# Turning 13 normalised tiles as squares on VectorE, with a trip through DRAM, instead of on TensorE

## The reference, cut to what matters

```python
# x (2048, 512) float32, adj (2048, 2048)
n = layernorm(x)
q, k, v = n @ W_q.T + b_q, n @ W_k.T + b_k, n @ W_v.T + b_v
z = (q @ k.T) / sqrt(512) * adj
attn = softmax(where(z == 0, -10000, z), axis=1)
x = x + relu(attn @ v)
m = layernorm(x)                       # the rows that the change is about
r = softmax(m @ Wr)                    # router, 8 experts; the two best are kept
w = softmax(top_2(r))
shared = (silu(m @ Wg_s) * (m @ Wu_s)) @ Wd_s
special = sum over the 2 picked experts e of w_e * (silu(m @ Wg[e]) * (m @ Wu[e])) @ Wd[e]
out = x + shared + special
```

## Time and profile before

| what | us |
|---|---|
| median of 3 runs | 1375.9 |
| the profiled execution's own time | 1377.3 |
| its span, first to last instruction | 1375.6 |
| TensorE busy | 1365.6 |
| TensorE weight loads | 1177.3 |
| VectorE busy | 909.2 |
| ScalarE busy | 453.6 |
| GpSimd busy | 196.9 |

### The profile page before, as it was taken

How to read it: one execution, slowest core, us unless ns; L and a number is a source line. 1 busy time by engine, 2 the same in 40 slices (tenths; PEclk the granted TensorE clock), 3 DMA queues, 4 the chain that set the end, 5 groups by cost and what they waited for, 6 DMA issues and landing times.

```text
span 1375.6 us, 19783 instructions
## 1 busy us (share of the span) xinstructions
PE 1365.6 (99%) x6720; PEld 1177.3 (86%) x6720; DVE 909.2 (66%) x1957; ACT 453.6 (33%) x702; POOL 196.9 (14%) x234
## 2 busy tenths in 40 slices
PE   9999999999999999999999999999999999999998
PEld 7888888888888878898989889898898989888887
DVE  7957767767777767465576747566475736367874
ACT  4522212212212245342343424234242525243331
POOL 3500112212211321011011110201102020100000
PEclk9999999999999999999999999999999999999999
DMA  5916565466466564462616133361435252553101
GB/s 183 259 46 169 163 185 165 148 187 168 153 175 191 175 237 147 154 175 55 206 31 215 31 106 124 54 207 34 124 107 152 83 155 98 148 151 107 47 16 61
DMA packets 114420, 185.47 MB, mean 135 GB/s; under 512 B 13776, under 2 KB 47568, under 8 KB 114336
## 3 DMA queue, kind: packets, MB, share of 16 engines
q1 hardware_dynamic: 98064, 153.43, 35.5%
q0 software_dynamic: 9760, 18.93, 7.0%
q10 hardware_dynamic: 6528, 12.22, 3.1%
HBM read 129.82 MB, written 55.77 MB: 135 GB/s over the span
## 4 chain that ended last, share of the span: by engine, by line
PE 91%; DVE 3%; DMA 3%; issue 2%; ACT 1%; SPq 0%; POOL 0%; DVEq 0%; ACTq 0%; POOLq 0%
PE bank L307 83%; PE bank L1042 5%; DMA turned<-p_moved 1%; DMA p_moved<-turned 1%; PE bank L874 1%; PE bank L1033 1%; DMA early_x<-x2t 0%; ACT sc L1210 0%; PE bank L798 0%; PE bank L752 0%; DVE fill L1602 0%; DVE pT_l L1457 0%; PE bank L868 0%; DVE turned L1620 0%; SPq L459 0%
## 5 line engine op out<-in xcount | busy, mean ns | idle before, releaser
L1846 DVE TENSOR_TENSOR hid<-bank,hid 128x384 f32<-128x384 f32 (+1 forms) x80 | 46.8, 584 | 176.6 <-PE bank L307 176.4
L307 PE MATMUL bank<-dn_h,hT_h 128*128 128x512 f32 x320 | 125.7, 393 | 0.2 <-DVE hT_l L1457 0.2
L307 PE MATMUL bank<-dn_h,hT_l 128*128 128x512 f32 x320 | 125.7, 393 | 0.0
L307 PE MATMUL bank<-dn_l,hT_h 128*128 128x512 f32 x320 | 125.6, 392 | 0.0
L307 PE MATMUL bank<-xq_h,gate_h 128*128 128x384 f32 (+1 forms) x320 | 111.3, 348 | 0.1
L307 PE MATMUL bank<-xq_h,gate_l 128*128 128x384 f32 (+1 forms) x320 | 111.2, 348 | 0.0
L307 PE MATMUL bank<-xq_l,gate_h 128*128 128x384 f32 (+1 forms) x320 | 110.8, 346 | 0.0
L307 PE MATMUL bank<-xq_h,up_h 128*128 128x384 f32 (+1 forms) x320 | 110.7, 346 | 0.0
L307 PE MATMUL bank<-xq_h,up_l 128*128 128x384 f32 (+1 forms) x320 | 110.4, 345 | 0.0
L307 PE MATMUL bank<-xq_l,up_h 128*128 128x384 f32 (+1 forms) x320 | 110.4, 345 | 0.0
L1128 ACT ACTIVATE hT_h<-hid 128x384 fp32r<-128x384 f32 (+1 forms) x96 | 53.8, 561 | 164.2 <-DVE hid L1846 124.7
(11 more groups left out here) (278 smaller groups left out, 3294.8 us busy)
## 6 DMA issues: line engine op xcount, KB each, us to landing
gate_raw<-in_L_ffn_Wg_dram SPq DMA_DIRECT2D x16, 1024.0 KB, 5.5
up_raw<-in_L_ffn_Wu_dram SPq DMA_DIRECT2D x16, 1024.0 KB, 10.2
dn_raw<-in_L_ffn_Wd_dram SPq DMA_DIRECT2D x16, 1024.0 KB, 12.5
sc<-in_adj_dram SPq DMA_DIRECT2D x30, 512.0 KB, 6.1
p_moved<-turned SPq DMA_DIRECT2D x30, 512.0 KB, 3.0
turned<-p_moved SPq DMA_DIRECT2D x120, 128.0 KB, 5.4
x_t<-in_x_dram SPq DMA_DIRECT2D x24, 256.0 KB, 4.8
slots<-x2row ACTq DMA_DIRECT2D x12, 512.0 KB, 4.4
```

Of the source, the lines that this page charges most:

```text
L307: mm = pe.matmul(o, lhs(a, c), rhs(b, c), start=first and n == 1, stop=last and n == 3 * len(chunks))
L1846: dve.tensor_tensor(hid[:, c % 2, 0:w], bank[2 + c % 2][:, 0:w], hid[:, c % 2, 0:w], ALU.mult).then_inc(sem("hid"), 1)
```

## The change

For the 13 tiles that steps 1 to 13 finish, TensorE's four transposes and the copy out of bank 7 go. In their place:

- VectorE turns each 32x32 square of `x2row` in place of its own (`turn_row`, one 128x512 transpose instruction), behind `row_normalised`, into `x2_squares`;
- SP stores `x2_squares` to DRAM (`x2_moved`), waits until it has landed and until x1 is stored, and reads it back in four DMAs with the squares in transposed order into `x2_banks` (`move_rows`);
- ScalarE copies `x2_banks` into `x2T` (`join_turned`): before the exponential in odd steps, behind it in even ones.

The logits on TensorE go behind the first `attend` group in odd steps and behind the second in even ones. On VectorE, `logits` in even steps goes behind the second `scaled_queries`, and `picks` behind the last `queries_low`; in odd steps the first `low` goes ahead of `ranks` and the first `fill_zeros`. The store of `x2T` goes from `store` into `move`, between the stores and the reads of the probabilities. In step 14 `picks` goes ahead of `first_pieces` on VectorE. In step 15 `count_picks` goes behind the first `attend` and `turn`, and VectorE's `residual` and `row_normalised` go ahead of `take_counts` and `ranks`. The last outputs share one semaphore.

```diff
 SP
-            def move(i):
+            def move(i, stored=False):
...
+                if stored:
+                    store_turned(i - 2)
                 for h in range(2):
                     sp.wait_ge(sem(f"p_half{h}"), MOVED * i + 16)
...
+            def move_rows(i):
+                sp.wait_ge(sem("row_turned"), i + 1)
+                sp.dma_start(x2_moved, x2_squares[:].rearrange("p a c q -> p (a c q)")).then_inc(sem("row_moved"), 16)
+                sp.wait_ge(sem("x1_out"), 16 * (i + 1))
+                sp.wait_ge(sem("row_moved"), MOVED * i + 16)
+                by_bank = x2_moved.rearrange("(i r) (a f) -> a r i f", i=BANKS, a=BANKS)
+                for a in range(BANKS):
+                    sp.dma_start(x2_banks[Q * a:Q * a + Q, :, :, :].rearrange("p i c q -> p i (c q)"), by_bank[a]
+                                 ).then_inc(sem("row_moved"), 16)
...
             def attention_step(i, b):
                 fetch(i, b)
+                stored = not isinstance(i, int) or i > 0
+                if stored:
                     store(i - 1)
-                move(i + 1)
+                    move_rows(i - 1)
+                move(i + 1, stored)
 TensorE
             def route_logits(i):
                 wait(pe, "x2T_done", i)
+                wait(pe, "counts_read", i - 1)
...
                 if last:
-                    count_picks(i - 1)
                     attend(i, 0, last)
                     turn(2)
+                    count_picks(i - 1)
...
-                if prev:
+                if split:
                     turn_normalised(i, b)
                 scores(i + 1, 1 - b, 3)
-                if prev:
+                if split:
                     route_logits(i)
...
                 attend(i, 0)
+                if prev and b == 1:
+                    route_logits(i)
                 attend(i, 1)
+                if prev and b == 0 and not split:
+                    route_logits(i)
 ScalarE
+            def join_turned(i):
+                wait(act, "row_moved", MOVED * i)
+                copy(x2T[:].rearrange("p c (i q) -> p i c q", q=Q), x2_banks[:]).then_inc(sem("x2T_done"), 1)
...
+                short = b == 1 or split
+                if split:
                     keep_turned(i)
+                elif prev and short:
+                    join_turned(i)
                 probabilities(i + 1, 1 - b)
-                if prev:
+                if prev and short:
                     router_exp(i)
+                if prev and not short:
+                    join_turned(i)
...
                 if prev:
+                    if not short:
+                        router_exp(i)
                     pick_exp(i)
 VectorE
+                wait(dve, "x2T_done", min(i - 1, ROWS) if isinstance(i, int) else i - 1)   # in output
...
+            def turn_row(i, b):
+                wait(dve, "x2_done", i)
+                wait(dve, "logits", i - 1)
+                wait(dve, "x2t_out", 16 * (i - 1))
+                dve.transpose(x2_squares[:], x2row[1 - b][:].rearrange("p (c a q) -> p a c q", a=BANKS, q=Q)
+                              ).then_inc(sem("row_turned"), 1)
...
                     row_normalised(i, b)
+                    if not split:
+                        turn_row(i, b)
...
+                if b == 1:
+                    low(i, 0)
                 if counted:
                     ranks(i - 1)
                 fill_zeros(i + 1, 1 - b, 0)
-                low(i, 0)
+                if b == 0:
+                    low(i, 0)
...
-                if prev:
+                short = b == 1 or split
+                if prev and short:
                     logits(i)
                 if ahead:
                     scaled_queries(2 * j + 2, 0)
                 if split:
+                    picks(i)
                     first_pieces(0, 2)
                 else:
                     turn_squares(i + 1)
                 if ahead:
                     queries_low(2 * j + 2, 0)
                     scaled_queries(2 * j + 3, 1)
-                if prev:
-                    picks(i)
+                if prev and not short:
+                    logits(i)
                 if ahead:
                     queries_low(2 * j + 3, 1)
+                if prev and not split:
+                    picks(i)
```

More of the change, by code:

```diff
@@ L61, in gnn_moe @@
     p_moved = nc.dram_tensor("p_moved", [2, P, BANKS * HALF * Q], F32, kind="Internal").ap()
+    x2_moved = nc.dram_tensor("x2_moved", [P, BANKS * D // BANKS], F32, kind="Internal").ap()
     x2t = nc.dram_tensor("x2t", [T, DC * P], F32, kind="Internal").ap()
@@ L93, in gnn_moe @@
         x2T = at("x2T", 194 * K, [P, DC, P])
+        x2_squares = at("x2_squares", 194 * K, [P, BANKS, DC, Q])
+        x2_banks = at("x2_banks", 192 * K, [P, BANKS, DC, Q])
         x2row = [at("x2row0", 196 * K, [P, D]), at("x2row1", 200 * K, [P, D])]
@@ L262, in gnn_moe @@
         LAST_O = bank[3]
+        ROWS = NT - 3
         TURNED = 2 * (NT - 1)
@@ L464, in store, with store_turned @@
                 sp.dma_start(rows(acc, i), x1[:]).then_inc(sem("x1_out"), 16)
+            def store_turned(i):
                 sp.wait_ge(sem("x2T_done"), i + 1)
@@ L469, in attention_step @@
                 fetch(i, b)
-                if not isinstance(i, int) or i > 0:
+                stored = not isinstance(i, int) or i > 0
+                if stored:
                     store(i - 1)
-                move(i + 1)
+                    move_rows(i - 1)
+                move(i + 1, stored)
             move(0)
@@ L481, in _ @@
             store(NT - 3)
+            store_turned(NT - 3)
             def load_turned(o, b, name):
@@ L520, in _ @@
             store(NT - 2)
+            store_turned(NT - 2)
             sp.wait_ge(sem("attended"), 4 * NT)
@@ L526, in _ @@
             store(NT - 1)
+            store_turned(NT - 1)
             sp.wait_ge(sem("sent"), 64 * NT)
@@ L618, in _ @@
                     sp.wait_ge(sem("z_done"), 4 + 4 * n + k + 1)
-                    sp.dma_start(rows(out, 8 + 4 * n + k), z[:, n, k, :]).then_inc(sem(f"out{n + 1}"), 16)
-            sp.wait_ge(sem("out"), 16)
+                    sp.dma_start(rows(out, 8 + 4 * n + k), z[:, n, k, :]).then_inc(sem("out"), 16)
+            sp.wait_ge(sem("out"), 16 + 2 * 64)
             sp.wait_ge(sem("out0"), 64)
-            sp.wait_ge(sem("out1"), 64)
-            sp.wait_ge(sem("out2"), 64)
         @block.gpsimd
@@ L1222, in last_group @@
                 copy(pT["h"][:, 4 * g:4 * g + 4, :].rearrange("p k q -> p (k q)"), bank[4 + g % 2][:]).then_inc(sem("pT_h"), 1)
+            def join_turned(i):
+                wait(act, "row_moved", MOVED * i)
+                copy(x2T[:].rearrange("p c (i q) -> p i c q", q=Q), x2_banks[:]).then_inc(sem("x2T_done"), 1)
             def keep_turned(i):
-                wait(act, "x2_turned", i)
+                wait(act, "x2_turned", i - ROWS)
                 wait(act, "logits", i - 1)
@@ L1322, in next_tokens @@
                     if b < 2:
-                        act.wait_ge(sem("x2_turned"), NT + q + 1)
+                        act.wait_ge(sem("x2_turned"), NT - ROWS + q + 1)
                         copy(o[:, :, part], bank[(c + 1) % 2 if b == 0 else 7][:].rearrange("p (c q) -> p c q", c=DC)).then_inc(sem("xq_h"), 1)
@@ L1656, in row_normalised @@
             def row_normalised(i, b):
-                wait(dve, "x2_turned", i - 2)
+                if isinstance(i, int) and i - 2 > ROWS:
+                    dve.wait_ge(sem("x2_turned"), i - 2 - ROWS)
+                else:
+                    wait(dve, "row_turned", i - 2)
                 normalise(x2row[1 - b][:], x1[:], NT + i, 1 - b).then_inc(sem("x2_done"), 1)
+            def turn_row(i, b):
[4 more added lines that the diff above has]
+                              ).then_inc(sem("row_turned"), 1)
             def logits(i):
@@ L1717, in attention_step @@
                     output(i, b)
+                    residual(i, b, j + b)
                     take_counts(i - 1)
+                    row_normalised(i, b)
                     ranks(i - 1)
-                    residual(i, b, j + b)
                     last_group(2)
-                    row_normalised(i, b)
                     last_group(3)
```

1 line of the change is left out of this document (removed).

## The result

The changed kernel takes 1379.2 us in the median (16 runs, 1378.3 to 1382.2), beside 1376.55 for the kernel before in 16 runs (1374.7 to 1377.9). The ratio is 1.0021, with an interval of 1.0014 to 1.0028. It is 2.65 us slower where 0.6 faster was forecast, so 3.25 us of the forecast have to be explained. The forecast was 1375.3, with a range of 1372.5 to 1378.5, and was set against the 1375.9 that three runs of the kernel before had given; its median of 16 is 0.65 higher. The profiled execution took 1378.7 with a span of 1377.0, that is 1.4 more than before in both.

What follows compares the result with a forecast made beforehand. TensorE was taken to bound the kernel, with VectorE at 97% of the bound and taking over after the change. +1.7 + 0.9 - 1.9 - 1.3 = -0.6 us gave 1376.7 profiled, 1375.3 in the runs' measure, range 1372.5 to 1378.5.

Steps and rivals of the forecast that it cites:

- who becomes the bound: Attention loop: VectorE becomes the bound, its pair of steps 53.37 us against 52.87 before, TensorE's 51.75.
- The turn: VectorE in each loop step: the added transpose costs 0.75 us, bounds 0.55 and 0.9; two make 1.5 a pair.
- The late logits of even steps: VectorE in even steps: small reads and picks no longer fill waits, costing 0.80 us, bounds 0.35 and 1.1.
- the number 51.07 for VectorE alone: Attention loop before the change: VectorE's pair without its waits for TensorE, 52.87 - 1.8 = 51.07 us.
- in odd steps the first `low` only changes places: 0 on VectorE: VectorE in odd steps: moving the first low part of the probabilities costs 0 us, lower bound -0.2.
- until the output at 175.66 its slack covers the additions, and TensorE's saving of about 0.9 shows: First loop steps: VectorE's slack of 1.66 us covers additions of 1.55, so TensorE's saving of about 0.9 shows.
- the end: Step 14 to the experts: picks save 1.9 us, the x2T store adds 0.9, no half clock saves 1.3.
- I take no fall: TensorE near 490: standing about 1.4 us does not lower its clock, so the half-clock stretch goes.
- The second, probabilities too late in odd steps: Rival, 18%: odd steps' `low` waits for late probabilities, some 5 us on top of the forecast, 1380.3 us.
- The third: Rival, 5%: x2T in odd steps later than 16 us after the output makes TensorE the bound again; 1382.3 us.
- The first, that VectorE doesn't take over: Rival, 25%: most of TensorE's 7.6 us saving comes through; 1365.1 us, or about 1370.5 with a 52.3 us pair.
- TensorE's idle of some 8 us: Sign in the attention: TensorE's idle rises to some 8 us, at odd steps' logits or at the outputs' release.

Runs made afterwards that it cites:

- double_turn: The changed kernel, with VectorE making each of the 13 transposes twice; 1389.0 us, 1.0094 of the kernel before.
- more_tensor: The changed kernel, with four unread TensorE transposes of a constant added in each of steps 1 to 13; 1379.8 us, 1.0024 of the kernel before.
- picks_first: low_back, with even steps' logits ahead of the first `queries_low`, `picks` ahead of the second, `router_exp` between ScalarE's two `queries`; 1375.1 us, 0.9982 of the kernel before.
- low_back: The changed kernel, with the odd step's first `low` back behind `ranks` and the first `fill_zeros`; 1377.0 us, 1.0002 of the kernel before.
- end_alone: The kernel before, with only the change's edits to steps 14 and 15; 1373.8 us, 0.9973 of the kernel before.
- after: The changed kernel as first profiled, against the kernel before; profiled execution 1378.7 us, median 1379.2, ratio 1.0021.
- odd_alone: The changed kernel with only odd steps' seven tiles turned the new way, even steps' the old, `low` at its old place; 1378.3 us, 1.0006 of the kernel before.
- odd_keep: odd_alone, with ScalarE's copy into x2T between the two high parts of the probabilities in even steps; 1370.8 us, 0.9954 of the kernel before.

## Why the prediction was wrong

**Right: who becomes the bound.** The mechanism of the forecast came true, and double_turn and more_tensor show it from both sides. The turn costs VectorE 0.76 us: before, the mask started 0.09 ahead of the end of x2row, now it starts 341.32 - 340.65 = 0.67 behind it; 0.75 was forecast. The late logits of even steps cost 0.79: from the queries (384.04) to the picks (386.22) it is 2.18, less 0.60 for the low part that now stands there, less the 0.79 from 328.19 to 328.98; 0.80 was forecast. Behind this stood the number 51.07 for VectorE alone. It closes: 53.60 less 1.42 for two turns (double_turn), less 0.52 (picks_first), less 0.25 (low_back) is 51.41, and the two reads of the logits and the new wait (0.35 + 0.06, from the rows) bring it to 51.0; with the first turns at their 0.76 it is 50.9.

**Wrong, the first failed step: "in odd steps the first `low` only changes places: 0 on VectorE".** It cost 0.23 us in each odd step; I had 0 and a bound on the side of a gain only. I had priced the instruction and not its neighbours. Whether an operation overlaps the one in front depends on what that is: the same `fill` starts 0.08 before the end of a low part and 0.12 after the end of an accumulator's reading. With the 0.06 of the new wait, and the even step 0.05 shorter, this is the pair's 53.60 instead of 53.37.

**Wrong, the second: "until the output at 175.66 its slack covers the additions, and TensorE's saving of about 0.9 shows".** It implies an output at 174.8. It came at 175.34, without a wait for TensorE in front of it. TensorE's saving did not show in step 1 either: its next output came at 146.59, against 146.50 before. In step 2 the transpose itself waited 0.52 us (151.19) for the store of x2T to have left the SBUF; I had listed that wait in the diff and given it no price, though I had moved the store behind the reads of the rows. This closes step 2. Before, it took 29.16 us, with 1.66 of slack at the output and 0.85 at the second mask, which waited 0.76 there (I had counted only the first). That leaves 26.65; with 1.55 added and the wait of 0.52 it is 28.72, and it took 28.75. The first of the five pairs took 54.00, 0.4 more than the others, and the last odd step grew by 0.18 where I had nothing.

The sum for step 14's head is 0.6 + (268.41 - 5 x 53.37 = 1.6) + 0.2 = 2.3 above the forecast's 1.6 (1.7 with the added wait), and it came at +3.9. That lies inside the bounds that I had written down (-2.7 to +4.6); the terms that I had put at nothing all came out on the slow side.

**Right in size, wrong in its terms: the end.** From step 14's output to the experts I had 40.11 - 1.9 + 0.9 - 1.3 = 37.8, and it is 37.56. The runs take it apart. With the end's edits alone it is 36.19 (end_alone): 3.9 less, where I had 1.9 + 1.3 = 3.2. With the loop's edits on top and no slow stretch it is 36.44 (low_back): 0.25 more, where I had 0.9 for the store of x2T. The 0.9 had too little behind it: step 14's second high part came 0.5 later than before, but no less late in end_alone, where the store stood at its old place. The last 1.1 is between low_back and after, and here "I take no fall" of the clock failed: TensorE waited 1.70 us for x2T at 478.64, and the 3.4 us behind it ran at 0.50, which costs 1.6 at the rate of the matmuls there (0.43 apart instead of 0.23). That the total came near is luck: a saving too small, a cost too large and a fall left out.

I had only asked whether the old wait of TensorE at 490 would shrink. I had not asked what TensorE does in step 14 once VectorE is late. It goes ahead, and its copy stays where ScalarE's queue has it. The wait for x2T there follows this lead from run to run. With the turn 6.38 us after the output (end_alone) there is none; with 5.79 (odd_alone) it is 0.71, with 5.49 (picks_first) 1.09, with 5.40 (low_back) 1.14, with 4.57 (after) 1.70, with 4.56 (more_tensor) 2.13. The second high part starts at 8.05 to 8.46 in all of them. That the lead makes the wait is read from these six profiles; no run changes the lead alone. The Trainium skill's rule in "DMA: Bandwidth & Descriptors", section "Queues, rings and completion order", that each DMA engine takes descriptors in ring order, fits the store's landing, which went from 2.1 to 6.8 us; I had applied the rule to the rows alone. The late landing is what step 2's transpose waited for.

**The median.** 1.25 us of the miss is not in the two profiles. 0.75 of it is that the profiled execution of before lay above its median. The rest is scatter of the changed kernel, whose executions differ in how long they stay at the lower clock behind the waits for x2T (3.41 us in one profile at 480, 6.83 in the other, and the profile beside the forecast is the one with the shorter). low_back, picks_first and odd_keep have no such stretch in their profiles, and all their executions have a mean granted clock of 0.999 or more; double_turn, with waits for x2T of 1.5 to 1.9 us, has them in five steps and a mean of 0.99 to 0.997. That shorter waits are the reason is an argument from these profiles and not shown; low_back still waits 1.14 at that place.

**The rivals.** The second, probabilities too late in odd steps, did not occur. ScalarE had the first high part at 340.20, 3.66 us after the output, against 3.46 before, and `low` ran at 342.61 without a wait. The third didn't either: x2T was there at 348.26, 11.7 us after the output, where I had 13.9. The first, that VectorE doesn't take over, is excluded by more_tensor. Of the signs, TensorE's idle of some 8 us came (9.9 us of its weight loads' waits for x2T), but the long ones, 1.35 us and more, stand in even steps and in step 14, where I had looked for them in odd ones.

## What to carry to other kernels

When an engine stands at 97% of the bound, take its whole dependent chain over one period, subtract only its waits on others, and price each edit by the gap it makes or closes to both neighbours; an instruction moved without a change costs something if it leaves an overlap. Compare what is moved with the slack that is there: here half of the tiles fitted into it and all of them did not. On the engine that copies for the bound, put the copy ahead of whatever waits for a DMA. Where an edit makes one engine late, the other comes early: ask what that one will wait for at the next place where it leads. And time an edit's neighbours without it, since here 3.4 of the 6.4 us came from the end's edits alone.

## What the runs showed of the hardware

- A 128x512 fp32 transpose in 32x32 squares takes VectorE 0.71 us, and two in a row, with a wait of the second for the first, 1.46 (double_turn).
- Not every wait brings TensorE's clock down. After waits of 0.97 (327.81) and 1.70 us (478.64) about 3.4 us ran at 1.2 GHz; after 1.14 us in low_back, 1.11 in odd_alone's even step, and 1.64 in the setup of before, it stayed at 2.4. The same code can do both: in odd_alone it fell after 1.13 (137.74), in after it stayed behind a wait of 0.95 at 274.19, and in double_turn it stayed after 1.65 (223.10) and fell after 1.57 at the same place of the next pair. What tells them apart stays open.
- A 256 KB store landed in 2.1 us in the median in the kernel before, where it mostly had the time to itself, and in 6.8 in the median beside the traffic of the probabilities, though its size was the same.
